# Layer 1's units: SyncE issues the maximum row first and the ring of the unit two on behind it

## The reference, cut to what matters

```python
q = (query @ Wq.T).reshape(B, T, 2 * H, D).transpose(0, 2, 1, 3)      # 32 half heads of 8
k = (query @ Wk.T).reshape(B, S, 2 * H, D).transpose(0, 2, 1, 3)
v = (query @ Wv.T).reshape(B, S, H, 2 * D).transpose(0, 2, 1, 3)
attn = jax.nn.softmax(jnp.einsum('bhtd,bhsd->bhts', q * scaling, k) + causal, axis=-1)
attn = attn.reshape(B, H, 2, T, S)
attn = attn[:, :, 0] - lam * attn[:, :, 1]
out = jnp.einsum('bhts,bhsd->bhtd', attn, v)        # then an RMS norm per head, and Wo
```

## Time and profile before

| | |
|---|---|
| median of 3 runs | 2289.54 us (2276.5 to 2292.45) |
| profiled execution, its own time | 2289.04 us |
| its span, first to last instruction | 2287.3 us |
| mean granted TensorE clock | 0.960 |
| TensorE busy (matmul) | 2018.3 us, 88% |
| VectorE, ScalarE, GpSimd busy | 62%, 39%, 29% |

### The profile page before, as it was taken

How to read it: one execution, slowest core, us unless ns; L and a number is a source line. 1 busy time by engine, 2 the same in 40 slices (tenths; PEclk the granted TensorE clock), 3 DMA queues, 4 the chain that set the end, 5 groups by cost and what they waited for, 6 DMA issues and landing times.

```text
span 2287.3 us, 33198 instructions
## 1 busy us (share of the span) xinstructions
PE 2018.3 (88%) x11778; PEld 1447.6 (63%) x11874; DVE 1411.2 (62%) x3219; ACT 885.4 (39%) x1749; POOL 665.0 (29%) x831
## 2 busy tenths in 40 slices
PE   2389899998999889998999989998999999999888
PEld 1257567576666766676675766757666676667656
DVE  4565675756666666656757567575665667665664
ACT  2143352524524244333534335251452425433352
POOL 2332331413313233223323233141331323222331
PEclk8589999999999999999999999999999999999999
DMA  6812523244231532216331252324423253221630
GB/s 208 300 47 90 165 75 107 65 122 130 61 109 62 163 111 70 74 56 185 103 94 56 91 160 80 107 65 126 122 60 102 74 172 102 80 82 39 180 98 15
DMA packets 105604, 240.47 MB, mean 105 GB/s; under 512 B 17048, under 2 KB 27288, under 8 KB 105184
## 3 DMA queue, kind: packets, MB, share of 16 engines
q1 hardware_dynamic: 91184, 194.41, 28.5%
q0 software_dynamic: 14256, 43.94, 6.7%
HBM read 179.67 MB, written 57.82 MB: 104 GB/s over the span
## 4 chain that ended last, share of the span: by engine, by line
PE 62%; DMA 11%; SPq 7%; DVE 7%; issue 3%; ACT 3%; POOL 0%; ACTq 0%; DVEq 0%; POOLq 0%
PE bank L420 20%; PE bank L582 12%; PE bank L503 11%; PE bank L469 8%; DMA qring<-mneg 7%; PE bank L519 5%; SPq L378 5%; DMA upring<-up_img 3%; PE bank L601 2%; DVE nmax L760 2%; PE bank L476 2%; DMA k_img<-probs 1%; ACT probs L660 1%; SPq L361 1%; ACT shared L630 1%
## 5 line engine op out<-in xcount | busy, mean ns | idle before, releaser
L420 PE MATMUL bank<-xnT,upring 128*128 128x512 f32 (+1 forms) x2208 | 721.8, 413 | 27.8 <-DMA upring<-up_img 27.6
L660 ACT ACTIVATE probs<-bank 128x512 f32<-128x512 f32 (+1 forms) x752 | 407.2, 557 | 394.6 <-PE bank L503 370.8
L503 PE MATMUL bank<-qring,kring 128*128 128x512 f32 (+1 forms) x1056 | 439.1, 419 | 107.1 <-DMA qring<-mneg 65.3
L760 DVE TENSOR_REDUCE nmax<-bank 128x2 f32<-128x512 f32 (+3 forms) x544 | 354.1, 658 | 218.4 <-PE bank L476 204.2
L469 PE MATMUL bank<-kring,qring 127*128 127x512 f32 (+3 forms) x1536 | 449.4, 346 | 34.3 <-DMA kring<-k_img 24.3
L420 PEld LDWEIGHTS bank<-xnT,upring 128*128 128x128 f32 x2208 | 416.3, 198 | 88.9 <-issue 30.8
L757 DVE CUSTOM_DVE_ANT_0 bank<-bank,mask_strip 128x512 f32<-128x512 f32 (+1 forms) x512 | 320.1, 635 | 164.2 <-PE bank L469 162.8
L469 PEld LDWEIGHTS bank<-kring,qring 127*128 127x128 f32 x1536 | 276.6, 195 | 123.2 <-DMA kring<-k_img 26.6
L503 PEld LDWEIGHTS bank<-qring,kring 128*128 128x128 f32 x1056 | 205.6, 196 | 214.1 <-DMA kring<-k_img 74.4
L582 PE MATMUL bank<-wdown,hbuf 128*128 128x256 f32 x1408 | 327.5, 382 | 0.0
L582 PEld LDWEIGHTS bank<-wdown,hbuf 128*128 128x128 f32 x1408 | 260.2, 191 | 32.7 <-issue 1.7
(11 more groups left out here) (127 smaller groups left out, 1862.4 us busy)
## 6 DMA issues: line engine op xcount, KB each, us to landing
upring<-up_img SPq DMA_DIRECT2D x176, 512.0 KB, 4.7
q_img<-probs SPq DMA_DIRECT2D x96, 256.0 KB, 3.2
qring<-q_img SPq DMA_DIRECT2D x256, 64.0 KB, 2.1
kring<-k_img SPq DMA_DIRECT2D x64, 256.0 KB, 3.1
qring<-q_img SPq DMA_DIRECT2D x32, 384.0 KB, 4.7
k_img<-probs SPq DMA_DIRECT2D x48, 256.0 KB, 4.5
up_img<-hbuf POOLq DMA_DIRECT2D x22, 512.0 KB, 4.9
gring<-gate_img POOLq DMA_DIRECT2D x32, 256.0 KB, 3.8
```

Of the source, the lines that this page charges most:

```text
L420: last = nc.tensor.matmul(out_ap, part_a(a, pa, k), part_b(b, pb, k), start=(n == 0), stop=(n == len(steps) - 1))
L503: nc.tensor.matmul(SC[n % 2][:, 0:heads * w].rearrange("p (g n) -> p g n", g=heads), kring[l][:, ks, kt * P:(kt + 1) * P], qring[l][:, s, ...
L660: nc.scalar.activation(pr, pr if biased else scores, ACT.Exp, scale=scale).then_inc(s_exp, 1)
L760: nc.vector.tensor_reduce(nmax[:, u % 2, g0:g0 + heads, qt], MX[n % 2][:, 0:heads * w].rearrange("p (g n) -> p g n", g=heads), AX.X, ALU.m ...
```

## The change

In `rest_of_unit` the two blocks change places: `max_row(sp, u + 1)` now stands ahead of the wait for `s_sc` and of `ring_load(sp, u + 2)`. Nothing else changes.

```diff
                     j = TILE_AFTER[u]
                     if j + 2 < J_ALL:
                         up_load(sp, j + 2)
+                    if not last_of_layer(u):
+                        max_row(sp, u + 1)
                     if not last_of_layer(u) and not last_of_layer(u + 1):
                         sp.wait_ge(s_sc, so_far(s_sc, PACKS * (u + 1)))
                         ring_load(sp, u + 2)
-                    if not last_of_layer(u):
-                        max_row(sp, u + 1)
```

## The result

The changed kernel takes 2431.72 us (median of 4 runs, 2424.13 to 2440.16), the one before 2286.56 us in the same comparison: a ratio of 1.0643, 95% interval 1.0609 to 1.0677. It is 6.4% slower. The forecast was 2437.

What follows compares the result with a forecast made beforehand. TensorE, busy 88%, was taken as the bound, waiting at unit heads for ring and row. Longer waits 116.6, contention -10 and clock +42 gave 148.6 us on 2289: 2437 us, range 2385 to 2475.

Steps and rivals of the forecast that it cites:

- The later of ring and row decides, and the ring becomes late: At 48 unit heads TensorE waits for both transfers; `kring` would land at 561.84, TensorE starting 2.5 us later.
- the rival by which the row alone decides: At unit heads TensorE does not need the ring; moving the row first gives 2224 us; chance 4%.
- The shift of 2.48 us per boundary: At 48 boundaries the ring lands later and TensorE waits longer: 116.6 us in all after taking off 2.4.
- contention term: `kring`, issued later, may miss the gate loads on POOL's queue: 0 to 21 us saved, -10 taken.
- the rival that had it at 6.8 us: At 40 boundaries the up tile directly behind slows `kring`'s landing; up to 148 us more, 2585 us; chance 6%.
- TensorE's clock: Longer idle at unit heads drops TensorE to 1.2 GHz: 36 falls, 30 more than now, 1.41 us each, +42 us.
- Row alone: 2.43 us: At boundaries, the row issued with no ring in front lands about 2.4 us later, as into unit 11.
- 0.25 us is all that the row loses behind the ring: On SyncE before the change, the finished row stood ready only 0.25 us before issue, its whole loss there.
- Nothing else waits: The 512 KB up tile load behind the ring is read over 20 us away; only TensorE waits for rings: nothing.

Runs made afterwards that it cites:

- e1: Kernel before, with SyncE waiting for the copied maxima ahead of the ring load and the row still behind the ring: 2406.57 us, ratio 1.053.
- e2: Changed kernel plus ten matmuls with unread results at the head of units 5 to 10, ahead of the ring wait: 2386.96 us, ratio 1.0451.
- e6: Kernel before, with `kring` issued first in the ring, the four `qring` pieces behind it and the row still last: 2262.49 us, ratio 0.9916.
- e4: Kernel before, with ScalarE issuing the rows of units 5 to 11 behind its own copy, SyncE only loading: 2295.88 us, ratio 1.0043.

## Why the prediction was right, step by step

- *The later of ring and row decides, and the ring becomes late.* Right. The wait changed its name to `kring`, at exactly 48 places; e1 shows the loss without the row in front; the rival by which the row alone decides would have made the changed kernel faster, and e1 has 120 of the 145 us of the loss with the row where it was.
- *The shift of 2.48 us per boundary.* Right in mechanism, 13 us too large with its contention term. I had +107 us for the waits and it is +94. Four sizes were off, in means over the 48 boundaries. The ring's first piece is issued 2.67 us later, not 2.54: between the row's issue and that piece SyncE spends 0.18 us, not 0.04 (it passes the waits of L312 there). The five issues take 0.18 longer, not 0.10. `kring` lands in 2.8 us in the mean, at the first boundaries of the batches too, where it took 3.4 in the mean of all 48 before and 4.5 at the first ones: 0.57 less, 27 us, when I had put at most 21 on that and taken 10. And TensorE starts 0.04 us behind `kring`'s landing, not 0.14; before, with the row landing last, it was 0.36 behind it. Two slips in the sum are small: 561.98 - 559.47 is 2.51, not 2.48, and the row landed later than usual behind `kring` at four boundaries, not three. An up tile 0.47 us behind `kring` did not slow it, which ends the rival that had it at 6.8 us.
- *TensorE's clock.* Right in sign and nearly in count: 33 falls in 48, forecast 36. The size was off: I priced all at 1.41 us, but 12 of them last longer and cost 2.5, so the term is +50, forecast +42. One basis was also read wrong: I wrote that no fall followed an idle below 2.15 us, and one did at 1.80. e2 confirms the term by taking 45 us away. By the rule of the Trainium skill (TensorE: Matmul & The Clock Gate, "HAM oscillation — how this bites in real kernels") waits of some 3 to 5 us are followed by a fall every time. The trace bears that out for the longest only: of the 48 idles, 2.8 to 4.8 us, the 13 longer than 3.55 us were all followed by a fall, but only 20 of the 35 others.
- *Row alone: 2.43 us.* Wrong, it is 1.8. The boundary of rows 8 was a bad sample: in the kernel before the row into unit 11 landed in 1.8 us in six of the eight batches, and in 2.43 and 2.66 in the other two; what lay beside it there is not shown. It was also wrong that 0.25 us is all that the row loses behind the ring: it lands besides 1.0 us later after its issue (2.80 for 1.82), as e6 shows. This changed nothing in the sum, as after the change no head waits for the row. The Trainium skill's 2.0 us (DMA: Bandwidth & Descriptors, "Anatomy of one DMA — SWDGE (gpsimd) path"), which the prediction quotes, was nearer.
- *Nothing else waits.* Right: the wait for up tiles (L420) is 27.1 us, before 27.6, and the tiles of L405 land in 3.9 us in the median where they took 4.6.

The errors of the two terms, 13 us too much and 8 too little, cancel in part; that the sum came to within 6 us of the measured time owes something to that.

## What to carry to other kernels

When a consumer waits for two transfers at one place, the waits view names only the one that came last; before moving it forward, look up when the other one landed: if that was 0.14 us before it, as here, 0.14 us is all that moving the named one can gain. A wait placed ahead of independent issues in one engine's program delays them all: count everything behind it. And within a group of transfers that is awaited as a whole, try the largest first; here it gave 0.8%.

## What the runs showed of the hardware that was not expected

- An 8 KB transfer landed in 1.8 us with nothing directly ahead, 2.35 behind a 64 KB piece, 2.8 behind 256 KB, and 3.1 when another engine issued it while the 256 KB were under way (medians over the 48 boundaries of the changed kernel, e6, the one before and e4).
- An idle TensorE costs more than its idle time: 48 idles of about 3.3 us were followed by 33 falls to 1.2 GHz worth some 50 us, and ten useless matmuls per head got 45 us back. Which of equal idles is followed by a fall I could not tell from the rows: 2.97 us before the score at 586.00 was, and 3.01 before the one at 602.08 was not.
